# GpSimd rounds with a converting copy, and the middle loop is written out, in a two-layer attention kernel

## What is computed

```python
# layer 0
theta, phi, g = (conv1x1(x, w, b) for w, b in (theta, phi, g))        # each 128 x 1024
attn = softmax(theta^T phi)                                           # 1024 x 1024
y = (attn @ g^T).reshape(8, 128, 32, 32)                              # no transpose before the reshape
x = (1 - w) * x + w * conv1x1(y, wz_w, wz_b)                          # "z" in the kernel
# layer 1
q, k = Wq x + bq, Wk x + bk                                           # 16 x 1024
v = Wv x + bv                                                         # 128 x 1024
out = gamma * (v @ softmax(q^T k / 4)^T)
fused = Wf @ concat(out, x) + bf                                      # "f" in the kernel
```

## Time and profile before

| | |
|---|---|
| runs | 540.46 us median (540.21 to 540.64) |
| profiled execution | 540.45 us |
| its span, first to last instruction | 538.6 us |
| busy | PE 519.5, PEld 436.6, DVE 415.9, ACT 371.5, POOL 303.0 us |
| granted TensorE clock | full speed throughout |
| DMA | 14.46 MB, mean 27 GB/s |

### The profile page before, as it was taken

The page is one execution under the profiler, slowest core; times in us unless marked ns, Lnnn a source line. Parts: engine busy times, 40 slices in busy tenths (PEclk is TensorE's granted clock), DMA queues, the critical chain, the costliest instruction groups (busy, mean ns, idle before and its releaser), DMA issues.

```text
span 538.6 us, 9732 instructions
## 1 busy us (share of the span) xinstructions
PE 519.5 (96%) x2933; PEld 436.6 (81%) x2933; DVE 415.9 (77%) x617; ACT 371.5 (69%) x668; POOL 303.0 (56%) x288
## 2 busy tenths in 40 slices
PE   7898899999999999999999999999999999899996
PEld 5677778888888888888888888888888887687886
DVE  5947677697787977788877888679778787888873
ACT  4765478658775688657876588765877557787763
POOL 1576266695277753865457852679527770364442
PEclk9999999999999999999999999999999999999999
DMA  5010000011000110002000030001200010000011
GB/s 180 17 40 2 5 6 0 2 40 65 6 22 0 43 59 5 19 0 97 10 0 19 0 102 5 0 19 32 70 5 19 1 39 30 1 3 29 1 40 39
DMA packets 6550, 14.46 MB, mean 27 GB/s; under 512 B 1280, under 2 KB 1792, under 8 KB 6528
## 3 DMA queue, kind: packets, MB, share of 16 engines
q1 hardware_dynamic: 6384, 14.05, 7.7%
q10 hardware_dynamic: 144, 0.13, 0.1%
HBM read 8.93 MB, written 4.19 MB: 24 GB/s over the span
## 4 chain that ended last, share of the span: by engine, by line
PE 83%; ACT 7%; DVE 4%; issue 3%; POOL 1%; DMA 1%; ACTq 0%; DVEq 0%
PE trans L501 18%; PE accum L525 10%; PE accum L527 10%; PE accum L526 10%; PE scores L491 5%; PE scores L465 5%; PE scores L467 5%; PE scores L466 5%; PE misc L552 3%; PE misc L465 3%; PE misc L467 3%; PE misc L466 3%; ACT probs L637 3%; ACT pt_hi L646 2%; PE misc L557 1%
## 5 line engine op out<-in xcount | busy, mean ns | idle before, releaser
L767 DVE TENSOR_TENSOR pt_lo<-trans,pt_hi 128x512 fp32r<-128x512 f32 x256 | 164.8, 685 | 66.3 <-ACT pt_hi L646 64.1
L646 ACT ACTIVATE pt_hi<-trans 128x512 fp32r<-128x512 f32 x256 | 138.9, 596 | 71.8 <-PE trans L501 70.6
L757 DVE TENSOR_REDUCE neg_max<-scores 128x1 f32<-128x1024 f32 x128 | 155.5, 1215 | 1.1 <-PE scores L467 1.1
L637 ACT ACTIVATE probs<-scores,neg_max 128x1024 f32<-128x1024 f32 x128 | 143.7, 1123 | 4.9 <-DVE neg_max L757 4.5
L501 PE MATMUL trans<-ident,probs 128*128 128x128 f32 x1024 | 134.3, 274 | 6.5 <-ACT probs L637 5.9
L501 PEld LDWEIGHTS trans<-ident,probs 128*128 128x128 f32 x1024 | 115.5, 141 | 19.5 <-ACT probs L637 8.2
L525 PE MATMUL accum<-pt_hi,g_hi 128*128 128x512 f32 x136 | 54.4, 400 | 0.0
L527 PE MATMUL accum<-pt_hi,g_lo 128*128 128x512 f32 x136 | 53.5, 393 | 0.0
L526 PE MATMUL accum<-pt_lo,g_hi 128*128 128x512 f32 x136 | 53.3, 392 | 0.0
L465 PE MATMUL scores<-phi_hi,theta_hi 128*128 128x512 f32 x112 | 49.0, 437 | 0.2 <-POOL phi_lo L883 0.2
L870 POOL TENSOR_TENSOR theta_hi<-proj_full,zero 128x512 fp32r<-128x512 f32 x14 | 14.5, 1039 | 60.9 <-ACT proj_full L665 60.9
(11 more groups left out here) (158 smaller groups left out, 1019.6 us busy)
## 6 DMA issues: line engine op xcount, KB each, us to landing
x_keep<-x_dram SPq DMA_DIRECT2D x8, 512.0 KB, 3.2
out_dram<-o_sb SPq DMA_DIRECT2D x15, 256.0 KB, 2.1
x_raw<-x_tiles_dram SPq DMA_DIRECT2D x7, 512.0 KB, 3.6
k_op<-k_op SPq DMA_DIRECT2D x12, 64.0 KB, 2.0
x_raw<-x_tiles_dram SPq DMA_DIRECT2D x2, 256.0 KB, 3.8
w_all<-weights_t_dram SPq DMA_DIRECT2D x1, 336.0 KB, 3.7
out_dram<-o_sb SPq DMA_DIRECT2D x2, 128.0 KB, 1.9
w_all<-weights_t_dram ACTq DMA_DIRECT2D x1, 128.0 KB, 3.8
```

The lines of the kernel that those rows point to most:

```text
L637: nc.scalar.activation(probs[:, k % 2, :], scores[:, k % 2, :], ACT.Exp, bias=neg_max[:, k % 4:k % 4 + 1], accum_out=row_sum[:, slot(gb), ...
L646: nc.scalar.activation(pt_hi[:, gb % 2, 4 * bank:4 * bank + 4, t * P:(t + 1) * P], trans[:, cols(bank)].rearrange("p (n q) -> p n q", n=4) ...
L757: nc.vector.tensor_reduce(neg_max[:, k % 4:k % 4 + 1], scores[:, k % 2, :], AX.X, ALU.max, negate=True).then_inc(max_ready, 1)
L767: nc.vector.tensor_tensor(pt_lo[at], trans[:, cols(bank)].rearrange("p (n q) -> p n q", n=4), f(pt_hi[at]), ALU.subtract).then_inc(pt_lo_r ...
```

## The change

`round_to` uses a converting copy instead of adding a broadcast zero; the tile of zeros, its memset and its semaphore go. `steps` emits the 5 trips of the middle loop one after the other, with constants in the waits, through an integer subclass that keeps the same choices of waits as in the loop. Order, tiles, matmuls and DMAs are the same.

```diff
+class Trip(int):
+    pass
...
-        zero = sb("zero", [P, 1])
...
-        zero_ready = sem("zero_ready")
...
         def groups(group, it):
             n = ORDER[group]
-            if not isinstance(it, int) and n < LOOP_GROUPS:
+            if isinstance(it, Trip) and n < LOOP_GROUPS:
...
             for k in range(LOOP_FROM):
                 emit(k, 0)
-            with engine.Fori(0, LOOP_TRIPS) as it:
+            for trip in range(LOOP_TRIPS):
                 for k in range(LOOP_FROM, LOOP_FROM + PERIOD):
-                    emit(k, it)
+                    emit(k, Trip(trip))
             for k in range(LOOP_TO, LAST_STEP):
                 emit(k, 0)
...
-                    if h == 1 and not isinstance(it, int):
+                    if h == 1 and isinstance(it, Trip):
...
-            nc.gpsimd.memset(zero[:, :], 0.0).then_inc(zero_ready, 1)
             nc.gpsimd.memset(ident[:, :], 0.0).then_inc(ident_ready, 1)
-            pool.wait_ge(zero_ready, 1)
 
             def round_to(hi, full):
-                return nc.gpsimd.tensor_tensor(hi, full, zero[:, :].broadcast_to([P, full.shape[1]]), ALU.add)
+                return nc.gpsimd.tensor_copy(hi, full)
...
-                    if n > 1 or not isinstance(it, int):
+                    if n > 1 or isinstance(it, Trip):
```

## The result

The changed kernel takes 537.96 us (median of 6 runs, 537.85 to 539.43) beside 540.55 us for the kernel before, timed alongside. The ratio is 0.9949 with a 95% interval of 0.9932 to 0.9967, so 0.5% faster. Run again, it took 538.13 beside 540.43 (0.9959, 0.9946 to 0.9972), a gain of 2.3 us.

A forecast was written before the change was run, and what follows sets the result against it. TensorE's own instruction stream was taken to bound the kernel. The copy's 0.80 us plus the loop's 0.40 made 1.20 us off 540.45, so 539.25 us, in a range of 538.6 to 540.5.

The forecast's parts named there:

- The bound and the cover: Whole kernel: TensorE's own instruction stream bounds it, busy 96% of the span; other engines count only where TensorE waits.
- The price of the copy: GpSimd's converting copy over 512 columns: 640 ns against the addition's 1040, taking GpSimd from 303 to about 261 us busy.
- y and phi, 0.40 us each: Two late GpSimd splits, at 66.71 and 94.61 us: the faster copy wins 0.40 us at each, 0.80 in sum.
- Nearly all of this lies beside TensorE's work and is worth nothing.: GpSimd's 42 us of saved work: worth nothing except at the splits of y and phi.
- That happens once in each trip.: Middle loop, exp to TensorE's transposes: constants in the waits save 0.08 us in each of five trips, 0.40 us.
- upper bound of 0.16 us a trip: Middle loop: the most to win if all TensorE idle time of a trip went, 5 x 0.16 = 0.8 us.
- The start, at 0: Zero tile's memset and wait removed: worth 0, hidden by GpSimd's 5.8 us wait for the weights' DMA.
- (c): Unrolled middle loop: late instruction fetches, 12 more packets of queue 8, make the kernel slower, 541.8 us; chance 0.07.
- (d): Four back edges of the loop: each holds TensorE for one fetch, 4.2 us together, giving 535.1 us; chance 0.04.
- low end of my range: Whole kernel: upper bounds of both gains, 540.45 - 0.94 - 0.8 = 538.7, with 0.1 for the spread of runs.

The follow-up runs named there:

- hold run: Loop written out, additions kept, GpSimd's first split of g waiting until VectorE has split wqk, against the kernel only written out: 538.53 us beside its 539.37.

## Why the prediction was right and wrong

- **The bound and the cover.** Right. TensorE's stream bounds the kernel, and 96 of 99 larger copies brought nothing.
- **The price of the copy.** 640 ns forecast, 615 measured; GpSimd 261 us forecast, 257.6 measured.
- **y and phi, 0.40 us each.** Right: 0.43 and 0.42, and they add up as argued, since what follows hangs on TensorE.
- **"Nearly all of this lies beside TensorE's work and is worth nothing."** This step failed for the first split of g, 0.44 us. I looked for GpSimd's effect only in the waits, and a hold inside a VectorE instruction isn't a wait: it stands in the trace as a long instruction. Its sign was there: four equal multiplications of 16 columns take 1.29 us, where one subtraction over 512 columns takes 0.69. The hold run shows the cause.
- **"That happens once in each trip."** The mechanism was right, and it is TensorE's own arithmetic; the term was mis-sized. The wait's extra time isn't paid in the long stall alone (0.07 us) but also where TensorE gets to the transposes of the other unit about on time (0.04 to 0.05), and with small change at other places it is 0.15 us a trip, 0.6 to 0.8 in all, where I had 0.40. My upper bound of 0.16 us a trip held, but by luck: TensorE's idle time in 64 us fell only from 0.16 to 0.09 us, and the other half came out of time that the view counts as busy.
- **The start, at 0.** I gave the code's length no effect outside the loop. The first DMAs land about 0.4 us earlier with TensorE's written-out program; 0.46 us of it was kept in the profiled execution and 0.19 in the repeat, some 0.3 by the medians. The cause is open.
- **Rivals.** (c) The fetches cost nothing that shows: 12 more packets of queue 8, as counted, 7 of queue 14, which I hadn't counted, and trips of equal length. (d) Nothing at the edges: the four other engines' back edges are worth 0.0 us, and TensorE's gain lies at its waits, not at its edges. The low end of my range left no room for a gain at a place I hadn't seen.

The sum of parts in the trace of the changed kernel: 0.44 + 0.43 + 0.42 for the copy, 0.75 for the trips, 0.46 for the start, 2.5 us; the profiled executions differ by 2.50. In the repeat it is 0.42 + 0.43 + 0.42 + 0.80 + 0.19 = 2.3, and they differ by 2.32.

## What to carry to other kernels

Where an engine is saturated, don't ask how much work a change takes off its neighbours, but at which single moments it waits for them; here three copies out of 115 were worth as much as all. Among those moments are instructions that are long for their size: compare equal instructions of one line by minimum and maximum, since a hold at a shared resource never shows as a wait. In a loop with register waits, count each place where a saturated engine meets another's result about on time, not only the long stall. And follow a head start at the beginning of a kernel to the end before you book it.

## What the hardware showed that I had not expected

- A VectorE multiplication of 128x16 fp32 from SBUF to SBUF took 160 ns alone and 1060 ns beside a GpSimd subtraction, until that one ended.
- A wait for a register's count costs TensorE 0.08 us more than one for a constant at the moment of release (0.12 against 0.04 us), and nothing measurable on the other four engines here.
- A TensorE program written out five times over fetches its code at no visible cost, and the first DMAs of the kernel land 0.4 us earlier with it than with the loop (VectorE's first work on them at 4.07 against 4.46 us on average over 8 and 5 profiles), for a reason that is open.
- In 7 of 14 profiles the first matmuls on real data, between one and eleven of them, took about 0.2 us longer to the next than in the others (0.43 against 0.23), differently from one execution of the same kernel to the next. Eleven of them cost 2 us.
